# Which pairs of score banks ScalarE fills ahead of the matmuls: the even ones, with two exceptions, in place of the odd ones

## The reference, cut to what matters

```python
h = group_norm1(x, n2_g, n2_b)
N = H * W
q = conv1x1(h, q_w, q_b).reshape(B, C, N).transpose(0, 2, 1)
k = conv1x1(h, k_w, k_b).reshape(B, C, N)
v = conv1x1(h, v_w, v_b).reshape(B, C, N).transpose(0, 2, 1)
scale = C ** (-0.5)
attn = jax.nn.softmax(jnp.einsum('bnc,bcm->bnm', q, k) * scale, axis=-1)
out = jnp.einsum('bnm,bmc->bnc', attn, v)
out = out.transpose(0, 2, 1).reshape(B, C, H, W)
return x + out
```

## Time and profile before

| what | value |
|---|---|
| time, median of 3 runs | 2857.21 us (2855.27 to 2861.93) |
| the profiled execution, its own time | 2859.16 us |
| its span in the trace | 2857.2 us |
| PE busy | 2766.2 us, 97% |
| DVE busy | 2519.7 us, 88% |
| ACT busy | 2223.1 us, 78% |
| POOL busy | 1824.8 us, 64% |
| granted TensorE clock, mean | 0.99 |

### The profile page before, as it was taken

The page is one execution under the profiler, slowest core; times in us unless marked ns, Lnnn a source line. Parts: engine busy times, 40 slices in busy tenths (PEclk is TensorE's granted clock), DMA queues, the critical chain, the costliest instruction groups (busy, mean ns, idle before and its releaser), DMA issues.

```text
span 2857.2 us, 54567 instructions
## 1 busy us (share of the span) xinstructions
PE 2766.2 (97%) x19644; PEld 941.4 (33%) x19644; DVE 2519.7 (88%) x3183; ACT 2223.1 (78%) x2338; POOL 1824.8 (64%) x1479
## 2 busy tenths in 40 slices
PE   6689999999999999999988999999999999999998
PEld 4333333333333333333323333333333333333332
DVE  4489999999999999999767999999999999999994
ACT  4267888888888888888866788888888888888887
POOL 1246666666666666666664666666666666666666
PEclk9899999999999999999998999999999999999999
DMA  7402000000000000000001000000000000000000
GB/s 192 115 8 41 10 10 10 10 10 10 10 10 10 10 11 10 10 10 8 5 9 44 8 11 10 10 10 10 10 10 10 10 10 10 11 10 10 9 6 5
DMA packets 36089, 52.93 MB, mean 19 GB/s; under 512 B 7912, under 2 KB 34024, under 8 KB 35056
## 3 DMA queue, kind: packets, MB, share of 16 engines
q1 hardware_dynamic: 35824, 49.47, 7.1%
HBM read 21.13 MB, written 14.16 MB: 12 GB/s over the span
## 4 chain that ended last, share of the span: by engine, by line
PE 87%; DVE 8%; issue 3%; ACT 1%; DMA 0%; POOL 0%; POOLq 0%; SPq 0%; DVEq 0%; ACTq 0%
PE ps L944 39%; PE ps L935 32%; PE ps L951 11%; DVE mxp L757 4%; PE ps L1051 2%; DVE arena L780 1%; DVE ps L770 1%; PE ps L967 1%; ACT arena L529 0%; DVE ps L773 0%; DVE bn L856 0%; DVE arena L866 0%; DVE x_max L857 0%; PE ps L1028 0%; DMA QM<-arena 0%
## 5 line engine op out<-in xcount | busy, mean ns | idle before, releaser
L459 POOL TENSOR_TENSOR arena<-arena 128x512 f32<-128x512 f32 x1224 | 1558.3, 1273 | 799.2 <-ACT arena L529 720.3
L757 DVE TENSOR_REDUCE mxp<-ps 128x1 f32<-128x1024 f32 x1296 | 1575.9, 1220 | 172.3 <-PE ps L951 141.7
L529 ACT ACTIVATE arena<-ps,bnd 128x1024 f32<-128x1024 f32 x1296 | 1373.9, 1111 | 412.6 <-PE ps L935 389.6
L944 PE MATMUL ps<-arena 128*64 128x512 f32 x5184 | 1268.1, 605 | 1.0 <-ACT pvb L539 1.0
L935 PE MATMUL ps<-arena 64*128 64x512 f16 x7776 | 1055.1, 377 | 5.0 <-ACT ps L566 3.2
L773 DVE TENSOR_TENSOR ps<-ps,arena 128x512 f32<-128x512 f32 x1260 | 870.2, 691 | 72.4 <-ACT arena L529 71.1
L566 ACT ACTIVATE ps<-mseed 128x1024 f32<-128x1024 f32 x612 | 629.1, 1028 | 53.3 <-ACT arena L529 0.4
L951 PE MATMUL ps<-arena,QM 64*128 64x512 f16 x2592 | 500.9, 383 | 18.9 <-DVE mxp L757 10.3
L935 PEld LDWEIGHTS ps<-arena 64*128 64x128 f16 x7776 | 375.1, 94 | 424.1 <-issue 31.8
L944 PEld LDWEIGHTS ps<-arena 128*64 128x64 f32 x5184 | 310.8, 136 | 505.2 <-issue 349.5
L951 PEld LDWEIGHTS ps<-arena,QM 64*128 64x128 f16 x2592 | 124.7, 93 | 735.8 <-DVE mxp L757 632.5
(11 more groups left out here) (110 smaller groups left out, 692.4 us busy)
## 6 DMA issues: line engine op xcount, KB each, us to landing
arena<-arena SPq DMA_DIRECT2D x144, 64.0 KB, 2.0
arena<-in_x_rows SPq DMA_DIRECT2D x8, 816.0 KB, 10.0
xs<-in_x SPq DMA_DIRECT2D x4, 1152.0 KB, 15.5
f_scratch<-arena SPq DMA_DIRECT2D x32, 144.0 KB
f<-f_scratch SPq DMA_DIRECT2D x16, 288.0 KB, 8.2
x_scratch<-arena SPq DMA_DIRECT2D x4, 1152.0 KB, 13.6
QM<-arena SPq DMA_DIRECT2D x72, 64.0 KB, 2.0
xst<-x_scratch SPq DMA_DIRECT2D x72, 64.0 KB, 2.2
```

The source lines that it names most:

```text
L459: nc.gpsimd.tensor_tensor(accA[:, n % 2, :], accA[:, n % 2, :], e, ALU.add).then_inc(adda_free, 1)
L529: nc.scalar.activation(flat(E[:, slot_of(n % 2, p), :, :]), flat(ps[:, S_BANK + 2 * buf:S_BANK + 2 * buf + 2, :]), ACT.Exp, scale=bnd[:, 6 ...
L757: nc.vector.reduce_max(flat(mxp[:])[:, v:v + 1], flat(ps[:, bank:bank + 2, :]), AX.X).then_inc(mx_free, 1)
L944: a = nc.tensor.matmul(ps[C * t:C * t + C, ACC_BANK, :], V[:, t, p, :], E[:, slot_of(par, p), t, :], start=(p == 0), stop=(p == NPAIR - 1) ...
```

## The change

The table `FILLED` replaces the rule "odd pairs from 3". It holds 3, 4, 6, 8, 11, 12, 14, ..., 34: the even pair of each turn, but the odd one in the turn of pairs 2 and 3 and in that of pairs 10 and 11. The count stays 17. `seed` writes the pair's own banks, and `scores` of an even pair may now take a seed.

```diff
 AHEAD = 4
 ROW_SUMS = 6
+
+FILLED = tuple(p + (p in (2, ROW_SUMS + 4)) for p in range(2, NPAIR, 2))
...
         def is_seeded(b, p):
 
-            return b in SEEDED and p % 2 == 1 and p >= 3
+            return b in SEEDED and p in FILLED
...
-                nc.scalar.activation(ps[:, S_BANK + 2:S_BANK + 4, :], mseed[:, n % 2, :].unsqueeze(1).to_broadcast([P, 2, CH]), ACT.Copy
+                at = S_BANK + 2 * (p % 2)
+                nc.scalar.activation(ps[:, at:at + 2, :], mseed[:, n % 2, :].unsqueeze(1).to_broadcast([P, 2, CH]), ACT.Copy
                                      ).then_inc(seeded, 1)
...
-                        scores(par, p + 2, n0 + p + 1)
+                        scores(par, p + 2, n0 + p + 1, seeds_before(b, j, p + 3) if is_seeded(b, p + 2) else None)
                         scores(par, p + 3, n0 + p + 2, seeds_before(b, j, p + 4) if is_seeded(b, p + 3) else None)
```

## The result

The changed kernel takes 2888.08 us (median of 4 runs, 2886.39 to 2891.76) beside 2857.52 for the kernel before on the same chip: 1.0109 times as long, 95% interval 1.0093 to 1.0125. It is 30.6 us slower, where 8.6 were forecast, and outside the range given.

What follows compares the result with a forecast made beforehand. TensorE was taken to bound the kernel, with ScalarE's order mattering at block starts; 0.24 us in 34 blocks plus 0.24 twice in last blocks made 36 x 0.24 = 8.6 us, giving 2865.8 us, range 2861 to 2871.

Steps and rivals of the forecast that it cites:

- What bounds the kernel: Whole span: TensorE bounds, working 97%; ScalarE's order is on the path only at a block's start, a 0.06 us wait.
- the middle turns: Ordinary turns inside a block: stay 3.92 us, cost nothing; spare time goes from 0.34 to 0.32 us.
- turn 10: Turn behind the row sums: pair 11 known at 859.16, needed at 859.26; 0.10 us to spare, no cost.
- (a): Exponential behind a fill costs more than the trace's one case; with 0.15 us more, 2873 us; chance 0.08.
- (c): Middle turns get shorter as the fill moves off seams between visits and weighing; with 0.03 us a turn, 2851; chance 0.05.
- Turn 2: Near a block's start, after move_pv: odd scores wait for pair 3's exponential; loss 0.24 us in each of 34 blocks.
- the 0.14: Time in us from an exponential's end until TensorE sees it, taken from the step behind a fill.
- Rival (b): Turn 2's 0.24 us is made good in VectorE's reductions; time stays at 2857 to 2861 us; chance 0.09.
- The last blocks: Last block of each image: turn 10 loses 0.24 us, twice in all; nothing taken for later turns.
- start later ... I take nothing for both: Middle turns: VectorE's and GpSimd's sums of the odd pair start later by about a fill less 0.22 us; cost nothing.
- VectorE sees no change: Middle turns: visits lie between the same 14 matmuls, so VectorE is unaffected; no cost.

Runs made afterwards that it cites:

- e5: Kernel before with pair 4 seeded in place of pair 5, odd pairs elsewhere: 2864.99 us beside 2858.05, ratio 1.0023.
- e1: Changed kernel with pair 35 seeded in place of pair 34: 2862.86 us, ratio 1.0017 to the kernel before.
- e2: Kernel before with the last two seeded pairs, 33 and 35, replaced by 32 and 34: 2886.33 us, ratio 1.0094.
- e3: Changed kernel with VectorE's write_out one pair earlier, behind pair 31 instead of 32: 2864.55 us, ratio 1.0022 to the kernel before.
- e4: Kernel before with write_out moved from behind pair 32 to behind pair 31: 2888.16 us, ratio 1.0100.
- e6: Changed kernel with GpSimd's add of pair 34 covering 8 of 512 columns: 2864.37 us, ratio 1.0024 to the kernel before.
- e7: Changed kernel with a small GpSimd memset put ahead of its add of pair 34, nothing left out: 2865.13 us, ratio 1.0026 to the kernel before.

## Why the prediction was wrong

**What bounds the kernel, and the middle turns: right.** All middle turns stay at 3.92 us, and the waits that I computed as spare did stay hidden, turn 10 with its 0.10 us too (3.92 us in the changed kernel). Rivals (a) and (c) fall with that.

**Turn 2: the mechanism right, the size too large.** The exponential of pair 3 starts at 853.24, behind a fill of 852.28 + 1.03 = 853.31, so 0.07 before its end as forecast. The odd scores wait for it. ScalarE and TensorE, from windows cut at that place:

```profile
853.24 1.10 ACT L531 ACTIVATE arena<-ps,bnd 128x1024 f32<-128x1024 f32 x1
```

```profile
854.39 0.39 PE L938 MATMUL ps<-arena 64*128 64x512 f16 x2
```

It ends at 854.34 and TensorE starts at 854.39, 0.05 us later. The term that was mis-sized is the 0.14 that I took for this step from the end of a fill. With 0.05 the loss is 0.24 - 0.09 = 0.15 us, which the turns show (4.15 for 3.99), and 5.0 us in all for my 8.6. Rival (b) is refuted by e5: the wait isn't made good.

**The last blocks: turn 10 right in kind, the rest made good.** Turn 10 of image 0's last block takes 3.76 us (1448.70 to 1452.46) for 3.60 (1430.60 to 1434.20), so 0.16 more where 0.24 was forecast, by the same mis-sized 0.14. Turn 6 and five of the later turns are 0.06 to 0.10 us shorter each, which I had taken for nothing, and the block as a whole neither gains nor loses. Turn 10 of the changed kernel and the start of turn 12:

```profile
1448.70 1.74 PE L938 MATMUL ps<-arena 64*128 64x512 f16 x12
...
1452.46 1.47 PE L938 MATMUL ps<-arena 64*128 64x512 f16 x12
```

**The step that failed** is in "Middle turns": VectorE's sums and GpSimd's "start later ... I take nothing for both". For the odd pair that is right. For the even pair the add starts earlier, by the same 0.22 us that I had just subtracted for the exponential, and I followed it to no neighbour; "VectorE sees no change" holds for the visits alone. I compared VectorE with the release of its data in a middle turn, not with what GpSimd does beside it, and only in the kinds of turn that I had laid out: start, turn 10, middle. `write_out` stands in turn 32 alone. In its place the trace shows `write_out` 1.1 us longer and turn 32 longer by 0.82 us in 30 blocks, 24.6 us of the 30.6. Giving pair 34's fill back to pair 35 takes away 25 us (e1), and putting the last two fills on pairs 32 and 34 brings in 28 (e2), and e3, e4, e6 and e7 show that VectorE's `write_out` is held by GpSimd's running add. The direction came out as forecast, but mostly through a term that the forecast doesn't have; of its own term, turn 2, 5.0 us of 8.6 are there.

## What to carry to other kernels

A change that makes an engine earlier is not free for being early. Follow each release that moves to the engine that takes it, and look at what runs beside it at the new time, in the turns with an instruction of their own as well as in the middle ones; and look in the trace before for one instruction with two durations (0.476 and 1.397 us here), which says that its neighbour matters. Where GpSimd's adds read SBUF and a rare VectorE instruction is of a kind that is held here (two SBUF tensors, or this `tensor_scalar`), place it into a gap of GpSimd's rather than beside the start of its next one: 0.22 us decided over 0.82 us a block.

## What the runs showed that I had not expected

- Which of two colliding instructions waits was decided between 0.03 and 0.08 us. An add that starts, by the profile, 0.03 us after `write_out` still comes first (1.58 us for `write_out`); one that starts 0.08 after comes second (1.53 us for the add). The add that comes second ends 1.13 us after `write_out`, whether it started 0.08 us behind it (e7) or 0.24 (before).
- The held instruction's recorded duration holds its wait: no idle time is shown before it, VectorE reads as busy, 30 us more in all.
- In e7 a GpSimd memset of 0.10 us runs beside `write_out` and neither is held; it writes SBUF and reads nothing.
- From ScalarE's end to TensorE's start it takes 0.05 us behind an exponential into SBUF and 0.14 behind a fill into PSUM. Why they differ stays open.
